# Attention scores of all heads at once and the feed-forward a step later in a fused RWKV layer

## The reference

```
xx = concat(x[:, 1:2], x[:, :-1]) - x
r, k, v = (x + xx*mix_r) @ W_r.T, (x + xx*mix_k) @ W_k.T, (x + xx*mix_v) @ W_v.T
g = sigmoid((x + xx*mix_g) @ W_g.T)
scan over tokens, per head: state = state * w + k v^T ;  out = state r
y = (out * g) @ W_o.T
x = layernorm(x + layernorm(y) * ln_gamma + ln_beta)
gate, up = fp4(x) @ fp4(w_gate).T, fp4(x) @ fp4(w_up).T
h = silu(gate) * up
x = layernorm(x + fp4(h) @ fp4(w_down).T)
```

## Time and profile before

| | |
|---|---|
| median of 3 runs | 657.91 us |
| profiled execution | 656.57 us |
| its span, first to last instruction | 654.6 us |
| mean granted TensorE clock | 0.959 |
| PE busy | 569.1 us (87%) |
| VectorE busy | 510.9 us (78%) |
| ScalarE busy | 277.2 us (42%) |
| GpSimd busy | 330.4 us (50%) |

### The profile page before, as it was taken

How to read it: one execution, slowest core, us unless ns; L and a number is a source line. 1 busy time by engine, 2 the same in 40 slices (tenths; PEclk the granted TensorE clock), 3 DMA queues, 4 the chain that set the end, 5 groups by cost and what they waited for, 6 DMA issues and landing times.

```text
span 654.6 us, 14594 instructions
## 1 busy us (share of the span) xinstructions
PE 569.1 (87%) x5120; PEld 477.9 (73%) x5120; DVE 510.9 (78%) x1506; ACT 277.2 (42%) x637; POOL 330.4 (50%) x471
## 2 busy tenths in 40 slices
PE   1468589999999999999999999999999999987754
PEld 1356467888878888888888888888888888876643
DVE  2988667888878888888888888888788888778751
ACT  1235255444444455444445444444445544432211
POOL 2234344555555555555555555555565555544321
PEclk9687689999999999999999999999999999999896
DMA  7300000000000000000000000000000000000000
GB/s 191 102 2 1 9 10 3 1 18 17 19 17 18 18 17 19 18 17 18 17 11 9 17 18 19 18 17 17 18 18 18 9 11 10 9 10 10 9 9 20
DMA packets 14046, 13.13 MB, mean 20 GB/s; under 512 B 2576, under 2 KB 13712, under 8 KB 13968
## 3 DMA queue, kind: packets, MB, share of 16 engines
q1 hardware_dynamic: 13968, 12.13, 6.2%
HBM read 7.93 MB, written 4.19 MB: 19 GB/s over the span
## 4 chain that ended last, share of the span: by engine, by line
PE 79%; DVE 9%; ACT 5%; POOL 2%; issue 2%; DMA 1%; SPq 0%; DVEq 0%; POOLq 0%; ACTq 0%
PE bank L734 20%; PE bank L867 14%; PE bank L677 9%; PE bank L752 9%; PE bank L716 4%; PE bank L804 4%; PE bank L759 4%; PE bank L769 4%; PE bank L859 3%; ACT hq_t L591 3%; PE bank L704 2%; DVE mix L1044 2%; PE bank L694 1%; POOL rstd L353 1%; PE bank L814 1%
## 5 line engine op out<-in xcount | busy, mean ns | idle before, releaser
L371 POOL TENSOR_SCALAR_AFFINE_SELECT scores<-scores 128x512 f32<-128x512 f32 x128 | 89.0, 708 | 81.0 <-ACT scores L508 80.4
L867 PE MATMUL bank<-down_t,hq_t 128*128 128x256 f32 x384 | 94.1, 396 | 21.6 <-ACT hq_t L591 21.6
L353 POOL TENSOR_TENSOR rstd<-veps,neg_half 128x1 f32<-128x1 f32 x96 | 77.8, 810 | 66.9 <-DVE veps L994 66.1
L867 PEld LDWEIGHTS bank<-down_t,hq_t 128*128 128x128 f32 x384 | 72.0, 194 | 38.3 <-ACT hq_t L591 29.4
L1044 DVE SCALAR_TENSOR_TENSOR mix<-shift,mu,x_t 128x128 f32<-128x128 f32 x256 | 82.5, 374 | 2.6 <-POOL shift L380 2.6
L508 ACT COPY scores<-bank 128x512 f32<-128x512 f32 x128 | 68.8, 590 | 34.5 <-PE bank L677 32.7
L752 PE MATMUL bank<-mix,proj_t 128*128 128x128 f32 x512 | 70.2, 295 | 10.5 <-DVE mix L1044 10.5
L734 PE MATMUL bank<-gu_hi,xq_hi 128*128 128x352 f32 x256 | 68.4, 349 | 11.2 <-DVE late L1092 6.4
L380 POOL TENSOR_TENSOR shift<-x_t 128x256 f32<-128x256 f32 x32 | 20.1, 629 | 112.6 <-ACT x_t L529 111.3
L752 PEld LDWEIGHTS bank<-mix,proj_t 128*128 128x128 f32 x512 | 66.1, 209 | 12.1 <-DVE mix L1044 11.1
L677 PE MATMUL bank<-r_par,rv 32*128 32x256 f32 x512 | 72.5, 400 | 0.8 <-ACT scores L508 0.8
(11 more groups left out here) (123 smaller groups left out, 1160.2 us busy)
## 6 DMA issues: line engine op xcount, KB each, us to landing
x_tok<-in_L_attn_x_dram SPq DMA_DIRECT2D x32, 128.0 KB, 2.3
out_dram<-late_down SPq DMA_DIRECT2D x32, 128.0 KB, 1.7
late_down<-in_L_ffn_w_down_dram SPq DMA_DIRECT2D x1, 704.0 KB, 8.6
late<-in_L_ffn_w_gate_dram SPq DMA_DIRECT2D x1, 640.0 KB, 7.1
late<-in_L_ffn_w_up_dram SPq DMA_DIRECT2D x1, 640.0 KB, 7.3
scores<-in_L_attn_W_r_dram SPq DMA_DIRECT2D x1, 256.0 KB, 5.0
scores<-in_L_attn_W_v_dram SPq DMA_DIRECT2D x1, 256.0 KB, 5.3
scores<-in_L_attn_W_g_dram SPq DMA_DIRECT2D x1, 256.0 KB, 5.5
```

The source lines that it names most:

```text
L353: g.tensor_tensor(rstd[:, i:i + 1], veps[:, i:i + 1], neg_half, ALU.pow).then_inc((rstd_ready, x_rstd, y_rstd)[i], 1)
L371: g.affine_select(out=a, in_=a, compare_op=ALU.is_ge, fill=0.0, base=0, pattern=[[0, 4], [1, P]], channel_multiplier=-1).then_inc(s_masked, 1)
L867: mm = t_.matmul(B_PA[:, 0:C], hq_t[:, t.c % 2, j], down_t[:, j], start=(j == 0), stop=(j == NH - 1))
```

## The change

Scores: all four quads in one call, into four banks (B_PA, B_PB, B_S0, B_S1), after the outputs. The call therefore also waits until the projections of the next tile have been read out of B_PA and B_PB, by ACT and by `kd`. Feed-forward: its stages on the fast path have lags 6, 7, 8 rather than 5, 6, 7 (`FFN` = 1), so there are 32 + 8 steps; x1 and xq have eight slots. PE's order in a step: the hidden transposes now stand before the v transposes and the second half of `gate_up`, and the down product after it. VectorE: the rounding of x (lag 5) is interleaved with that of the hidden values; `kd` waits for the tanh and not for the finished sigmoid and stands before the last two hidden operations; the product with the gate (`attn`) moves to lag 3; the mixes come last. GpSimd: the masks stand together, behind the x scaling. Weights: first step first, then two pieces after each of steps 0 to 3; ACT copies the turned weights twice (`gu_hi` and `gu_full`), and `low_parts` reads them from SBUF. The first tile's x is transposed ahead of the tables.

```diff
-LAG_MAX = 7
+FFN = 1
+LAG_MAX = 7 + FFN
+        s_bank = (B_PA, B_PB, B_S0, B_S1)
...
-            def scores_of(t, half):
-                if half == 0:
-                    wait(pe, rv_ready, t.count(1, 1))
-                    wait(pe, r_par_ready, t.count(2, 2))
-                wait(pe, s_moved, t.count(QUADS, 2 * half))
+            def scores_of(t):
+                wait(pe, rv_ready, t.count(1, 2))
+                wait(pe, r_par_ready, t.count(2, 4))
+                wait(pe, tanh_ready, t.count(1, 2))
+                wait(pe, kd_ready, t.count(1, 2))
+                wait(pe, ln2_step, t.count(LN2, 1 - (5 + FFN) * LN2))
+                wait(pe, h_t_ready, t.count(2, -8 - 2 * FFN))
+                wait(pe, s_moved, t.count(QUADS, 0))
                 for hf in range(KC):
-                    for i in range(2):
-                        q = 2 * half + i
+                    for q in range(QUADS):
                         rows = slice(32 * q, 32 * q + 32)
-                        mm = t_.matmul((B_S0, B_S1)[i][:, hf * 256:hf * 256 + 256],
+                        mm = t_.matmul(s_bank[q][:, hf * 256:hf * 256 + 256],
...
-                        act.wait_ge(w_moved, n + 1)
+                        s.copy(gu_full[:, k, lo:hi], w_bank[n % 2][:, 0:hi - lo]
+                               ).then_inc(w_moved, 1)
...
+            def quantize(n, k):
+                w = pieces[n]
+                rows, cols = w.shape
+                if k == 0:
+                    wait(dve, q_ready, n - 3)
+                    if n in (0, 3):
+                        dve.wait_ge(*((gate_loaded, 16 * 2), (ffn_loaded, 16 * 3))[n // 3])
+                if k == 3:
+                    wait(dve, q_ready, n - 1)
+                grid(k, w, q_grid[0:rows, n % 2, 0:cols], cols // BLK, q_scale[:, n % 4],
+                     q_inv[:, n % 4], q_mag[:, n % 2], q_step[n % 2], lambda i: QN * (n // 2) + i)
...
+            def low_parts(m):
+                dve.wait_ge(w_moved, 9 + 4 * m)
+                for k in range(KC):
+                    cols = slice(m * HID, (m + 1) * HID)
+                    v.tensor_tensor(gu_lo[:, k, cols], gu_full[:, k],
+                                    gu_hi[:, k, cols].bitcast(F32), ALU.subtract
+                                    ).then_inc(gu_lo_ready, 1)
```

The moves inside the step functions, as the order of each engine's queue (- before, + after; H is `hgrid`, X is `xgrid`):

```
  TensorE, order in step:
-  x transposes, W_o, xq transposes, r/v, g/k, sums, scores 0-1, outputs, gate_up 0,
-  v transposes, scores 2-3, gate_up 1, hidden transposes, down
+  x transposes, W_o, xq transposes, r/v, g/k, sums, outputs, scores 0-3, gate_up 0,
+  hidden transposes, v transposes, gate_up 1, down
  VectorE, order in step (H = hgrid, X = xgrid):
-  attn, state sum, H0, half, state, u2, H1, n3.0, H2, n3.1, n1.0, xq_lo, mix R, n3.2, H3,
-  n1.1, mix V, n1.2, u1, H4, u, H5, n2.0, H6, n2.1, kd, n2.2, mix G, mix K, gated 0, X0-X6, gated 1
+  H0, H1, u2, H2, n3.0, n1.0, H3, X0, n1.1, n3.1, n1.2, n3.2, xq_lo, u1, H4, X1, u, kd, H5, X2,
+  n2.0, H6, n2.1, X3, n2.2, attn, state sum, gated 0, X4, mix R, half, X5, mix V, state, X6,
+  mix G, mix K, gated 1
  GpSimd, order in step:
-  shift, xb, rstd2, rstd0, mask 0, rstd1, mask 1, hq, gate_pow, masks 2-3, xq
+  shift, (weights scaling), xb, rstd0, rstd2, hq, rstd1, xq, masks 0-3, gate_pow
  ScalarE, order in step:
-  x_t, xq_hi, rv, r_par, tanh, sigmoid, scores 0-1, y_out, silu 0, x1, v_tok, scores 2-3, silu 1, hq_t
+  x_t, xq_hi, rv, r_par, tanh, sigmoid, y_out, scores 0-3, silu 0, hq_t, v_tok, x1, silu 1
```

More of the change, by code:

```diff
@@ L415, in step @@
                                     ).then_inc(gate_pow_ready, 1)
[L416 to L426, removed]
+                if general:
+                    scale_x(tile(4), general)
             def dequantize(n):
@@ L788, in step @@
                 t = tile(0)
-                if t is not None:
-                    wait(pe, x_in[t.c], t.affine(16, 16))
-                    wait(pe, x_moved, t.count(1, 0))
-                    wait(pe, v_tok_ready, t.count(1, -1))
-                    wait(pe, xq_t_ready, t.count(1, -5))
-                    for k in range(KC):
-                        mm = t_.transpose(B_T[:, k * P:(k + 1) * P],
-                                          x_tok[:, t.c, k * P:(k + 1) * P], ident)
-                    mm.then_inc(x_tr, 1)
+                if t is not None and not t.first():
+                    transpose_x(t, general)
                 t = tile(4)
@@ L861, in step @@
                     mm.then_inc(h_tr, 1)
-                t = tile(6)
+                t = tile(1)
+                if t is not None:
+                    wait(pe, rv_ready, t.count(1, 1))
+                    wait(pe, x_moved, t.count(1, 2))
+                    wait(pe, xq_t_ready, t.count(1, -3 - ffn))
+                    wait(pe, v_tok_ready, t.count(1, 0))
+                    for k in range(KC):
+                        mm = t_.transpose(B_T[:, k * P:(k + 1) * P], rv[:, t.c % 4, 1, k], ident)
+                    mm.then_inc(v_tr, 1)
+                t = tile(5 + ffn)
+                if t is not None:
+                    gate_up(t, 1, ffn)
+                t = tile(6 + ffn)
                 if t is not None:
@@ new lines, in early @@
+            def early(c, general):
+                if c == 0:
+                    dve.wait_ge(tabs_moved, 5)
+                for m in range(2):
+                    if c == 3 + m and not general:
+                        low_parts(m)
+                if c < 4 and not general:
+                    weights(2 * c)
+                if c == 0 and general:
+                    for n in range(0, len(pieces), 2):
+                        weights(n)
+                    for m in range(2):
+                        low_parts(m)
@@ L1093, in gated @@
                                     ).then_inc(hid_step, 1)
-                moves = t4 is not None and t4.c != TPB - 1 and not general
                 if t4 is not None and general:
```

416 lines of the change are left out of this document (216 added, 200 removed).

## The result

The changed kernel takes 625.71 us (median of four runs, 622.5 to 627.71) against 657.95 us for the kernel before (now four runs): a ratio of 0.949, interval 0.942 to 0.955. The forecast was 614, range 600 to 640; the direction and the range held, the middle was 12 us too low. The profiled execution took 623.75 us, its span is 622.0.

What follows compares the result with a forecast made beforehand. TensorE, almost back to back, was taken as the bound. Step 17.50 - 1.06 - 0.65 + 0.28 = 16.07 us; steady steps -51.8, head -1.2, tail +9.1 gave span 610.7, time 614.0 us, range 600 to 640.

Steps and rivals of the forecast that it cites:

- (a): Scores on TensorE: sixteen records in four row groups take 1.06 us instead of 2.12, saving 1.06 a step.
- Rival 1: Scores don't run four at a time, so their saving is 0: 648 us; chance 0.10.
- (b): ACT's copy before the down product runs beside TensorE, saving 0.65 us a step, at least 0.4.
- (c): Second gate/up half: TensorE stalls 0.28 us a step for silu and gated product, bounds 0.2 and 0.9.
- (d): VectorE's queue keeps up, idling some 2.7 us a step; interleaved roundings and early kd gain nothing.
- D: The end of the down product in a step, from which the prediction counted VectorE's times.
- (e): GpSimd's x scaling and masks have five us of slack, ACT's score copies end just in time; nothing added.
- Rival 3: Hidden rounding reaches GpSimd late behind kd and u, 0.9 us a step beyond slack: 636 us; chance 0.08.

Runs made afterwards that it cites:

- block runs: Changed kernel with the seven x rounding steps in one block behind the k mix, not interleaved: 647.7 us, ratio 0.984.
- the last version: Changed kernel with r mix and first silu early, v, g and k mixes ahead, norm step later and outputs halved: 608.6 us, ratio 0.926.
- the run with one wait of 1.7 us a step on TensorE: Kernel before, with hidden transposes ahead of v transposes and second gate/up half, and ACT's copy of them behind the first silu: 733.3 us, ratio 1.116.
- mixes-ahead run: Changed kernel with r mix and first silu early, and v, g and k mixes ahead of the last three x rounding steps: 615.9 us, ratio 0.934.

## Why the prediction was right, and where it was off

Direction: right, by the part that it named. (a) The scores of all quads cost 1.07 from start to start, forecast 1.06; the forecast rested on the fourfold start of the state products, and the run with the pairs kept apart puts a price on it: 1.1 us a step, 1.2 with its wait. Rival 1 is out.

(b) ACT's copy before the down product is hidden, as said: 0.7 us of idle in the whole run.

(c) The new wait for the gated product is 0.40, forecast 0.28. The hand-over from VectorE to TensorE was put at 0.05; it is 0.15 (gated product from 350.46 for 0.52, so to 350.98, next half at 351.13).

(d) is the step that failed: "VectorE so idles some 2.7 us a step and is not the bound", with u2 at 0.05 after D and a price of nothing for the interleaving. Two things were wrong in it. The durations were too short: 16.07 less 2.7 leaves 13.4 us of work, where the same instructions had filled 14.6 before, by the prediction's own figure, and fill 14.3 now (86.57 of 100). And it did not matter how much VectorE idled but where. 1.7 us of idle time lie ahead of the first gated product, where nothing stood that could use it, and behind that come the mixes. From the first gated product to the second the prediction had 3.6 us (10.5 to 14.1), four mixes among them; the trace has 4.8 (333.89, a step before the one shown at 350.46, to 338.71). The g and k mixes take 0.54 each, although the prediction itself put the masks beside them in (e); at 0.27 each these four alone would give 1.1 us of it back.

A row of the kernel before had shown this price. Eight mixes take 4.14 us in the head, while GpSimd scales weights until 28.20:

```profile
...
25.26 2.94 POOL L435 TENSOR_TENSOR late<-hq,q_scale 128x768 f32<-128x768 f32 x2 [1.49 <-DVE hq L912]
```

Two of the eight last until GpSimd's two instructions end, 1.58 and 1.14 us, and the six behind them come 0.26 apart. So here a mix pays by the GpSimd instruction that it meets, and the mean of 0.52 hides that.

In the changed kernel u2 came 1.2 us late (1.23 after the end of the down product, forecast 0.05), TensorE waited 0.41, and the masks-first and block runs show that further delay counts nearly whole. Rival 3 had the right kind of chain (VectorE's strict queue) at the wrong place: TensorE waited 0.3 us in 18 steps for the hidden scaling, and the run with the later kd shows room there, though ahead of the transposes it was 0.24 and not 0.6.

(e) held: neither masks nor ACT's copies made TensorE wait by their own lateness. What it missed is what the masks do to VectorE.

In sums: the step is 16.47 and not 16.07, 24 x 0.40 = 9.6 us; first down product at 122.78 and not 120, 2.8; the tail 103.9 against 2.9 + 102.2 = 105.1, 1.2 less. Together 11.2 of the 11.3 between 610.7 and the span of 622.0. The 0.40 is this: TensorE waits 0.79 a step (7.3, 6.8 and 0.3 us in 300) where 0.28 was forecast, 0.51 more, the residual sum's 0.41 and the gated product's 0.12 above all; and its work, the step without the waits, is 15.68 where 15.79 was forecast, 0.11 less. So a small part of the nearness is luck: a wait that was left out and work that was put too high lean against each other.

What stays open: which of the head's parts gave what, since head and tail were forecast as sums and no run took one of them alone; and why two halves of the last version, each worthless or worse alone, are worth 1.1% together was argued from the waits and not taken apart further.

## What to carry to other kernels

When a change fills the engine that binds, ask of the next engine not how much it idles in a step but where: idle time ahead of a wait is lost, and all that stands behind it is on the path. Put independent work there (here one pair of mixes, 10 us). And price an instruction of VectorE, or of GpSimd, by what the other does in the same moment: a reordering that lets the two overlap anew changes durations that were measured apart.

## What the runs showed of the hardware

VectorE's `scalar_tensor_tensor` on two SBUF operands (128x128, float32) takes 0.27 from start to start while GpSimd is idle and, as a mean of four, 0.54 while it scales and masks. The masks pay little, 2.56 for four against 2.40 beside other work. A product with one operand in PSUM (0.52) and a reduction (0.89) beside the same masks lose nothing. Two `tensor_scalar` instructions with one SBUF operand do lose: `x_mag` takes 0.74 against 0.29, and the step on 128x44 takes 0.54 against 0.18.

By the rule of the Trainium skill ("SBUF — State Buffer", "SBUF: two separate sides"), the two engines contend where VectorE's instruction is in a two-port mode, or where it has two SBUF inputs and GpSimd's reads SBUF. The traces agree for the mixes, the product and the reduction; whether the two `tensor_scalar` instructions run in such a mode no trace here shows. The page also says that the pair of ports is locked for a whole instruction and the other engine fully blocked. That fits VectorE's side: beside four masks of 0.64 each the mixes come near one to a mask, and in the head of the kernel before two mixes last as long as the two scalings that they meet.

On GpSimd's side it fits some instructions and not others. `shift` takes 0.61 where it meets nothing, and 1.29 in the mixes-ahead run, where a pass of VectorE over 704 columns with two SBUF operands had started 0.06 before it. A mask beside mixes is only 0.04 longer than elsewhere, though a mix of 0.27 passed with nearly each. The runs don't settle why the masks get off so lightly.

Row groups of TensorE worked side by side whatever the order in which their products were given, as long as no wait stood between: sixteen records in 1.16 us also when one pair of quads came wholly first.

In the run with one wait of 1.7 us a step on TensorE the granted clock was 0.92 to 0.95 through the steady part; it was 1.00 in the kernel before. The sum of the idle time does not go with it: with the masks first TensorE waited 1.4 and 0.4 a step and was busy 89.98 us of 100 (300 to 400 us), less than the 90.80 here, and its granted clock stayed at 1.00.
